# Decoder layer kernel: how the masks of the adapter attention are added, and in which order its passes run

## The chip, the core and the metric

The kernel runs on one core of one Trainium2 chip. The metric is the device time of one execution in microseconds (us). The kernel before takes 1193.47 us, the median of three runs (1193.44 to 1193.86).

## The reference

Three post-norm blocks over x, 16 sequences ("batches") of 128 tokens by 256 features, all in float32: layer A (causal self-attention with 16 heads), layer B (self-attention with 32 heads of 8 features under an additive mask, plus gated attention to a second input of the same shape), and block C/D (attention with 16 heads of 128, then four experts). The change touches layer B:

```
scores = (q @ k.T) * inv_sqrt_d + attention_mask      # mask: one 128x128 float32 array per batch, 0 or -1e9
scores = maximum(scores, finfo.min)
w = softmax(scores);  attn = w @ v
a = tanh(gate) * softmax(q @ a_k.T * inv_sqrt_d);  attn = attn + a @ a_v     # no mask here
x = layernorm(x + attn @ Wo)
```

## The kernel before

**Engines and waits.** Each engine runs a list of instructions written out in order (pe_ab, dve_ab, act_ab, pool_ab, sp_ab) and waits on semaphores. Nothing is reordered: the lists are generated by a loop over steps s, and tables (xts, projs, masked, clamps, ends, tos, turned ...) say in which step each piece of background work stands.

**Units and passes.** A unit is four heads: a score tile of 128 x 4 x 128 in one PSUM bank. Layer A has 64 units, layer B 256 (numbers n = 64 to 319). A batch of layer B has 16 units: eight of self-attention with the mask (kd = 0), then eight on the second input (kd = 1). Units go in pairs, one pair in every second step. In this text a step is named by s modulo 16, so a batch has the pair steps 0, 2, ... 14, and steps 0 to 6 hold its masked units in the first pass. Two batches make a chunk (number c); layer B has chunks 8 to 15.

*Pass 1* computes the scores on TensorE (L554) into bank 0 or 1 (bank n % 2), and VectorE takes the row maxima of each bank (`maxima`, L737). A unit's first write waits for the maxima two units earlier (m_dve). *Pass 2*, 28 steps later, computes the transposed scores with the maxima subtracted through extra rows of the operands (L589) into bank 2 or 3 (`bank2`). In masked units VectorE adds the transposed mask and writes the sum to SBUF (`mask2`, L746), and ScalarE takes the exponential there (L978); in the others ScalarE reads the bank (L985). `pv`, two steps after pass 2, multiplies by the values: 16 matmuls for a pair, each 32 columns wide, on four column tiles (L611).

**The mask.** A chunk's mask is loaded in float32, clamped (L729) and split into a high part (ScalarE, L963) and a rest (GpSimd, L1090). Pass 1 of a masked unit begins with two matmuls of a 128x128 identity by 512 mask columns (L547), one for each part. The mask turned by TensorE (L512) and copied by ScalarE (L935) serves `mask2`.

**Small products.** Turned maxima ("sh": L565, then the copy L971 by ScalarE), turned outputs ("to": L621, after the copy L997), projections and output products (L472 to L474) share banks 6 and 7 alternately from step s = 86 on: `home[key] = bank[6 + len(home) % 2]`. Before it writes, `turn` waits until the last user of that bank has been read.

**Order in a step.** TensorE: pass 1, pass 2, pv, small products. VectorE: maxima, divide (L766 to L777) and other outputs, L723, then the two `mask2`, then residual and statistics (L801, L695 to L699).

## Time and profile before

| what | value |
|---|---|
| median of three runs | 1193.47 us |
| profiled execution, first to last instruction (its own time) | 1193.7 us |
| TensorE busy in it | 1128.8 us (95%) |
| VectorE busy | 993.6 us (83%) |
| ScalarE, GpSimd busy | 660.4 us, 656.9 us (55% each) |
| mean granted TensorE clock | 0.990 |
| packets of the sync engine's DMA queue, share of 16 engines | 23.1% |

Layer A runs to about 175 us, layer B from there to about 556 us, C and D to the end. No time around the span is given for the profiled execution, so its span is its own time here. Matmuls are pipelined, and a listed duration of one contains a fixed part that overlaps with its neighbours: what a matmul costs in a row of them is the distance of starts. Idle time of an engine that nothing later waits for costs nothing.

### The profile page before, as it was taken

The page shows a single profiled execution, that of the slowest core. Times are in us where ns is not written, and L with a number is a line of the kernel's source. Part 1 is how long each engine was busy: PE and PEld are TensorE (multiplying, and loading weights), DVE is VectorE, ACT ScalarE, POOL GpSimd, SP SyncE. Part 2 cuts the span into 40 slices and gives each one's busy share as a digit, 9 for nine tenths or more (in the row PEclk, how much of TensorE's full clock was granted, in tenths as well). Part 3 has the DMA queues.
Part 4 walks back from the last instruction along what each step waited for, and adds up shares of the span by engine and source line. Part 5 has one row for each costly group of instructions (what it writes and reads, how often), then busy time and mean ns, then how long its engine had stood idle before and what let it go on. Part 6 is the DMA issues. An engine that isn't in the chain of part 4 may idle for free.

```text
span 1193.7 us, 29551 instructions
## 1 busy us (share of the span) xinstructions
PE 1128.8 (95%) x11172; PEld 934.4 (78%) x11172; DVE 993.6 (83%) x2284; ACT 660.4 (55%) x1687; POOL 656.9 (55%) x706
## 2 busy tenths in 40 slices
PE   5899999899999999879999999999999999999997
PEld 5667666666776766546899899998999899997887
DVE  6768887888889898978888888888888888877977
ACT  5466554566766667565555444444444444558663
POOL 4467655545455455254778544544554454847665
PEclk9899999999999999999999999999999999999999
DMA  6875443334333433212222000000000100101111
GB/s 161 205 186 135 122 125 87 87 95 116 88 106 101 106 97 97 76 58 76 68 63 63 1 1 2 1 1 2 1 1 1 37 1 1 37 18 37 36 36 36
DMA packets 98670, 76.68 MB, mean 64 GB/s; under 512 B 73547, under 2 KB 86987, under 8 KB 98529
## 3 DMA queue, kind: packets, MB, share of 16 engines
q1 hardware_dynamic: 98529, 74.80, 23.1%
q8 instruction: 89, 1.46, 0.5%
q14 instruction: 52, 0.43, 0.1%
HBM read 53.86 MB, written 19.92 MB: 62 GB/s over the span
## 4 chain that ended last, share of the span: by engine, by line
PE 58%; DVE 23%; issue 7%; ACT 5%; POOL 3%; SPq 2%; DMA 2%; DVEq 0%; POOLq 0%; ACTq 0%
PE bank L1518 5%; DVE B_nr L737 4%; PE bank L1519 4%; PE bank L1520 4%; PE bank L1574 4%; PE bank L1547 4%; PE bank L611 4%; DVE PT L746 3%; PE bank L472 2%; PE bank L554 2%; SPq L1154 2%; PE bank L1534 2%; PE bank L1589 2%; PE bank L1587 2%; PE bank L1588 2%
## 5 line engine op out<-in xcount | busy, mean ns | idle before, releaser
L1822 POOL TENSOR_TENSOR C_QK<-C_t1b,C_t2b 128x512 f32<-128x512 f32 x128 | 168.9, 1320 | 226.6 <-DVE C_t2b L1661 226.0
L1658 DVE SCALAR_TENSOR_TENSOR C_t1b<-bank,C_bcol,C_tabs 64x512 f32<-64x512 f32 x256 | 192.0, 750 | 37.3 <-PE bank L1520 33.2
L737 DVE TENSOR_REDUCE B_nr<-bank 128x4 f32<-128x512 f32 x256 | 164.4, 684 | 22.6 <-PE bank L554 21.0
L1518 PE MATMUL bank<-C_XTh,C_Wh 128*128 128x512 f32 x256 | 111.9, 437 | 4.4 <-DVE C_t2b L1661 1.9
L985 ACT ACTIVATE PT<-bank 128x512 f32<-128x512 f32 x160 | 92.2, 598 | 39.8 <-PE bank L589 39.3
L1754 ACT ACTIVATE C_P<-bank,C_nm 128x128 f32<-128x128 f32 x256 | 90.7, 367 | 34.0 <-DVE C_nm L1671 32.4
L978 ACT ACTIVATE PT<-PT 128x512 f32<-128x512 f32 x96 | 59.3, 630 | 88.7 <-DVE PT L746 88.7
L1773 ACT ACTIVATE C_V<-bank 128x512 f32<-128x512 f32 x64 | 38.1, 597 | 124.1 <-PE bank L1536 122.5
L611 PE MATMUL bank<-PT,vpool 128*32 128x128 f32 x2048 | 97.4, 285 | 4.3 <-ACT PT L978 3.1
L1519 PE MATMUL bank<-C_XTl,C_Wh 128*128 128x512 f32 x256 | 101.2, 395 | 0.0
L1520 PE MATMUL bank<-C_XTh,C_Wl 128*128 128x512 f32 x256 | 100.8, 394 | 0.0
L1661 DVE SCALAR_TENSOR_TENSOR C_t2b<-bank,C_bcol,C_tabs 128x512 f32<-128x512 f32 x128 | 96.1, 751 | 1.8
L554 PEld LDWEIGHTS bank<-stk 48*128 48x128 bf16 (+1 forms) x1280 | 50.9, 96 | 52.3 <-issue 27.5
L554 PE MATMUL bank<-stk 48*128 48x128 bf16 (+1 forms) x1280 | 77.7, 221 | 9.6 <-DVE B_nr L737 8.9
L589 PE MATMUL bank<-stk 54*128 54x128 bf16 (+1 forms) x1280 | 76.5, 219 | 10.0 <-DVE PT L746 3.8
L1762 ACT ACTIVATE C_OTh<-bank,C_bcol 128x512 fp32r<-128x512 f32 x64 | 44.1, 690 | 73.6 <-PE bank L1574 73.0
L1682 DVE SCALAR_TENSOR_TENSOR C_OTl<-bank,C_bcol,C_OTh 128x512 fp32r<-128x512 f32 x64 | 47.9, 748 | 38.9 <-ACT C_OTh L1762 38.8
L705 POOL TENSOR_TENSOR rstd<-ve,mhalf 128x1 f32<-128x1 f32 x48 | 28.1, 584 | 91.1 <-DVE ve L699 91.1
L589 PEld LDWEIGHTS bank<-stk 54*128 54x128 bf16 (+1 forms) x1280 | 53.5, 95 | 27.8 <-DVE PT L746 6.8
L1534 PE MATMUL bank<-C_Wh,C_XTh 128*128 128x256 f32 x256 | 72.5, 283 | 1.6 <-DVE C_t2b L1661 1.3
L1587 PE MATMUL bank<-C_Wh,C_OTh 128*128 128x256 f32 x256 | 72.0, 281 | 0.4 <-DVE C_OTl L1682 0.4
L1535 PE MATMUL bank<-C_Wl,C_XTh 128*128 128x256 f32 x256 | 71.9, 281 | 0.0
(267 smaller groups left out, 3683.5 us busy)
## 6 DMA issues: line engine op xcount, KB each, us to landing
Adrq<-PB SPq DMA_DIRECT2D x16, 192.0 KB, 3.2
Adrk<-PB SPq DMA_DIRECT2D x16, 192.0 KB, 3.4
...
```

Source lines behind the costliest of these rows:

```text
L554: m = e.matmul(bank[n % 2][:, j * 128:j * 128 + 128], QS[L][i3][rows, h, :], (AS if kd else KS[L])[i3][rows, h, :], start=bool(kd), stop=b ...
L589: m = e.matmul(bank2(n)[:, j * 128:j * 128 + 128], (AS if kd else KS[L])[i3][rows, h, :], QS[L][i3][rows, h, :], start=bool(L), stop=bool( ...
L611: m = e.matmul(o[32 * j:32 * j + 32, c3 * 128:c3 * 128 + 128], vp[:, h, :], pt_of(n)[:, j * 128:j * 128 + 128], start=first or not L, stop ...
L737: e.tensor_reduce(dst, bank[n % 2][:, :].rearrange("p (a b) -> p a b", a=4), AX.X, ALU.max, negate=True).then_inc(sem("m_dve"), 1)
L1518: e.matmul(o[:, :], CWh[hp][:, cs], XCh[0][:, t, :], start=t == 0, stop=False)
L1519: e.matmul(o[:, :], CWh[hp][:, cs], XCl[0][:, t, :], start=False, stop=False)
L1520: m = e.matmul(o[:, :], CWl[hp][:, cs], XCh[0][:, t, :], start=False, stop=t == 1)
L1534: e.matmul(ob, XCh[0][:, t, xs], CWh[hp][:, cs], start=t == 0, stop=False)
L1587: e.matmul(o, OCh[:, bs], CWh[hp][:, cs], start=r == 0 and b % 2 == 0, stop=False, skip_group_check=True)
L1658: e.scalar_tensor_tensor(out=v4(t1b[kq][lo:lo + 64, :]), in0=v4(o[hi:hi + 64, :]), scalar=bc[hi:hi + 64, :], in1=tabsC[hi:hi + 64, 2 * kq ...
L1661: e.scalar_tensor_tensor(out=v4(t2b[kq][:, :]), in0=v4(o[:, :]), scalar=bc, in1=tabsC[:, 2 * kq, :].unsqueeze(1).to_broadcast([128, 4, 128 ...
L1822: e.tensor_tensor(QK[v % 3][:, kq, :], t1b[kq][:, :], t2b[kq][:, :], ALU.add).then_inc(sem("rc_pool"), 1)
```

## The change

The mask of pass 1 is split into three bf16 parts (MQ) instead of two float32 parts. They are written to DRAM and read back by rows (MP): 96 partitions, three parts of 32 rows, four groups of rows. A unit's mask is then four matmuls with a 96x32 selection matrix (`pick`), each with 512 moving columns and each into its own 32 output partitions of the bank. The same is done with the three parts turned (MTQ, MTP) for pass 2, and only in the first unit of each pair (t = 0, even n). The odd unit (t = 1) is still added by VectorE. ScalarE now reads even masked units from the bank. The preparation of a chunk has two copies by ScalarE and two subtractions by GpSimd in place of one each, six more transposes on TensorE with a copy of 768 elements by ScalarE, and four DMAs. The turned maxima go in two DMAs for a batch instead of four.

From s = 64 on TensorE's order in a step is pv, mask of pass 2, masks of pass 1, pass 2, pass 1, small products. Pass 2 comes 26 steps after pass 1 instead of 28 and pv stays at 30. VectorE does `mask2` (odd unit) ahead of the maxima of the step. `mask_turns` puts the transposes of the mask parts ("mp") in step 5 for chunks 10 to 15, among the users of banks 6 and 7.

```diff
-    MKh = [sb(f"B_MKh{i}", [128, 2, 128], F32R, st_ab) for i in range(2)]
-    MKl = [sb(f"B_MKl{i}", [128, 2, 128], F32R, st_ab) for i in range(2)]
+    MP = [sb(f"B_MP{i}", [96, 4, 2, 128], BF16, st_ab) for i in range(2)]
...
+    pick = sb("B_pick", [96, 32], BF16, st_ab)
+    MQ = sb("B_MQ", [128, 3, 2, 128], BF16, st_ab)
+    MR = sb("B_MR", [128, 2, 128], F32, st_ab)
+    MTP = [sb(f"B_MTP{i}", [96, 4, 2, 128], BF16, st_ab) for i in range(2)]
+    MTQ = sb("B_MTQ", [128, 3, 2, 128], BF16, st_ab)
...
-    LAST_FIRST = 292
+    LAST_FIRST = 294
...
+    def is_masked(n):
+        return n >= NA and unit(n)[2] == 0
+
+    def adds_mask(n):
+
+        return is_masked(n) and unit(n)[3] == 1
...
-        return [s - 12] if 12 <= s < NA + 12 else pair(s - 28)
+        return [s - 12] if 12 <= s < NA + 12 else pair(s - 26)
...
+    mask_parts = [{s + k: c for s, c in clamps.items()} for k in (1, 2, 3, 4)]
+    masks_out = {s + 5: c for s, c in clamps.items()}
+    mask_turns = {s + (1 if c < 10 else 3): c for s, (c, _) in masked.items()}
+    masks_t_out = {bg0(c) + 28: c for c in range(8, 16)}
...
+        def mask_parts_turned(c):
+            q.wait_ge("mq_pool", 2 * (c - 7))
+            o = turn(("mp", c), "mt_act", 2 * (c - 7))[:, :].bitcast(BF16)
+            for part in range(3):
+                for b in range(2):
+                    k = 2 * part + b
+                    m = e.transpose(o[:, k * 128:k * 128 + 128], MQ[:, part, b, :], identb[:, :])
             m.then_inc(sem("mt_pe"), 1)
...
+        def mask_by_rows(o, parts, b):
+
+            for g in range(4):
+                e.matmul(o[32 * g:32 * g + 32, :].rearrange("p (a b) -> p a b", a=4), pick[:, :],
+                         parts[0:96, g, b, :].unsqueeze(1).to_broadcast([96, 4, 128]), start=True, stop=False, skip_group_check=True)
+
+        def mask1(n):
+            b = unit(n)[1]
+            c = 8 + b // 2
+            if n >= 2:
+                q.wait_ge("m_dve", n - 1)
+            q.wait_ge("ld_B", 48)
+            q.wait_ge(*parts_ready("mp_in", c))
+            mask_by_rows(bank[n % 2], MP[c % 2], b % 2)
+
+        def mask2(n):
+            b = unit(n)[1]
+            c = 8 + b // 2
+            bank2_free(n)
+            q.wait_ge("ld_B", 48)
+            q.wait_ge(*parts_ready("mtp_in", c))
+            mask_by_rows(bank2(n), MTP[c % 2], b % 2)
...
-                elif not kd:
-                    q.wait_ge("identr", 1)
-                    q.wait_ge("mkl_pool", b // 2 + 1)
-                    for k, part in enumerate((MKh, MKl)):
-                        e.matmul(scores, identr[:, :], part[(b // 2) % 2][:, b % 2, :].unsqueeze(1).to_broadcast([128, 4, 128]),
-                                 start=k == 0, stop=False, skip_group_check=True)
...
         for s in steps:
+            if s >= NA:
+                for n in pv_units(s):
+                    pv(n)
+                for n in pass2_units(s):
+                    if is_masked(n) and not adds_mask(n):
+                        mask2(n)
+                for n in pass1_units(s):
+                    if is_masked(n):
+                        mask1(n)
+                if pass2_units(s):
+                    pass2(pass2_units(s))
             if pass1_units(s):
                 pass1(pass1_units(s))
-            if pass2_units(s):
-                pass2(pass2_units(s))
-            for n in pv_units(s):
-                pv(n)
+            if s < NA:
+                if pass2_units(s):
+                    pass2(pass2_units(s))
+                for n in pv_units(s):
+                    pv(n)
...
             if s in CHANGE:
                 outputs()
+            for n in pass2_units(s):
+                if adds_mask(n):
+                    mask2(n)
             for n in pass1_units(s):
                 maxima(n)
...
-            for n in pass2_units(s):
-                if n >= NA and unit(n)[2] == 0:
-                    mask2(n)
...
+        def mask_part(c, part):
             q.wait_ge("clamp", c - 7)
-            if c >= 10:
-                q.wait_ge("s_pe", last_unit(2 * (c - 2) + 1, 0) + 1)
-            e.activation(MKh[c % 2][:, :, :], MK[c % 2], ACT.Copy).then_inc(sem("mkh_act"), 1)
+            if part == 0:
+                if c > 8:
+                    q.wait_ge(*parts_ready("mp_in", c - 1))
+                    q.wait_ge("mt_pe", 2 * (c - 8))
+                e.activation(MQ[:, 0, :, :], MK[c % 2], ACT.Copy).then_inc(sem("mq_act"), 1)
+            else:
+                q.wait_ge("mq_pool", 2 * (c - 8) + 1)
+                e.activation(MQ[:, 1, :, :], MR[:, :, :], ACT.Copy).then_inc(sem("mq_act"), 1)
...
+        def mask_out(c):
+
+            q.wait_ge("mq_pool", 2 * (c - 7))
+            q.wait_ge("mp_in", 32 * (c - 8))
+            load(mask_dram[0], MQ[:, :, :, :].rearrange("p j b k -> p (j b k)"), "mp_in")
...
+        def mask_rows(c):
+
+            q.wait_ge("mp_in", 32 * (c - 8) + 16)
+            if c >= 10:
+                q.wait_ge("s_pe", last_unit(2 * (c - 2) + 1, 0) + 1)
+            load(MP[c % 2][:, :, :, :].rearrange("p g b k -> p g (b k)"), by_rows(mask_dram[0]), "mp_in")
...
```

**TensorE, steps 4 and 6 of a batch, before.** B_nmb is the shift (maxima in parts), OTf the outputs to turn, B_MKh and B_MKl the mask parts, stk the operands of L554 (pass 1) and L589 (pass 2).

```order
L565 MATMUL bank<-identb,B_nmb 96x128 [waits ab_act,sh_pool]
L565 MATMUL bank<-identb,B_nmb 96x128
L621 MATMUL bank<-ident,OTf 128x128 [waits mt_act,ot_act]
L621 MATMUL bank<-ident,OTf 128x128 x2
L547 MATMUL bank<-B_MKh,B_identr 128x512 [waits m_dve]
L547 MATMUL bank<-B_MKl,B_identr 128x512
L547 MATMUL bank<-B_MKh,B_identr 128x512 [waits m_dve]
L547 MATMUL bank<-B_MKl,B_identr 128x512
L554 MATMUL bank<-stk 128x128 x8
L589 MATMUL bank<-stk 128x128 [waits e_act]
L589 MATMUL bank<-stk 128x128 x7
L611 MATMUL bank<-PT,vpool 32x128 x8
```

After the two turns come the masks, pass 1, pass 2 and pv of step 6.

**TensorE, the same place in the kernel after, in a batch that prepares a mask.** B_MQ are the mask parts to turn, B_MP those read back by rows; L641 is pass 2, L602 pass 1, L663 pv.

```order
L673 MATMUL bank<-ident,OTf 128x128 [waits mt_act,ot_act]
L673 MATMUL bank<-ident,OTf 128x128 x2
L543 MATMUL bank<-identb,B_MQ 128x128 [waits sh_act,mq_pool]
L543 MATMUL bank<-identb,B_MQ 128x128 x5
L663 MATMUL bank<-PT,vpool 32x128 x8
L560 MATMUL bank<-B_MP,B_pick 32x512 [waits m_dve]
L560 MATMUL bank<-B_MP,B_pick 32x512 x3
L560 MATMUL bank<-B_MP,B_pick 32x512 [waits m_dve]
L560 MATMUL bank<-B_MP,B_pick 32x512 x3
L641 MATMUL bank<-stk 128x128 [waits e_act]
L641 MATMUL bank<-stk 128x128 x7
L602 MATMUL bank<-stk 128x128 x8
```

The transposes of B_MQ stand between the turned outputs of step 4 and pv of step 6 and wait for ScalarE's copy of the turned maxima (sh_act), since they use the same bank; everything of step 6 has moved behind them, and pass 1 is the last of its step.

**VectorE, from the maxima of step 8 to the adds of step 12, before.** B_nr<-bank is the maxima of a pair, PT<-bank,stk and stk<-bank,stk are mask adds.

```order
L737 TENSOR_REDUCE B_nr<-bank 128x4 x2
L723 TENSOR_TENSOR XTl<-bank,XTh 128x512
L737 TENSOR_REDUCE B_nr<-bank 128x4 x2
L791 TENSOR_TENSOR OTl<-bank,OTh 128x256
L729 TENSOR_SCALAR stk<-stk 128x256
L737 TENSOR_REDUCE B_nr<-bank 128x4 x2
L746 TENSOR_TENSOR PT<-bank,stk 128x512 x2
```

**VectorE, the same place after.**

```order
L803 TENSOR_REDUCE B_nr<-bank 128x4 x2
L789 TENSOR_TENSOR XTl<-bank,XTh 128x512
L812 TENSOR_TENSOR PT<-bank,stk 128x512
L803 TENSOR_REDUCE B_nr<-bank 128x4 x2
L857 TENSOR_TENSOR OTl<-bank,OTh 128x256
L795 TENSOR_SCALAR stk<-stk 128x256
L812 TENSOR_TENSOR stk<-bank,stk 128x512
L803 TENSOR_REDUCE B_nr<-bank 128x4 x2
```

Each masked pair of pass 2 has one add instead of two; it stands between L789 (formerly L723) or L857 (formerly L791) and the maxima of its step.

## Rows read from the trace of the kernel before

**Rows 1.** The page: busy us (share of the span) and instructions by engine.
```profile
PE 1128.8 (95%) x11172; PEld 934.4 (78%) x11172; DVE 993.6 (83%) x2284; ACT 660.4 (55%) x1687; POOL 656.9 (55%) x706
```

**Rows 2.** Busy time by stretch: length, then busy us of each engine, clock, DMA.
```profile
386.70:429.80 43.10, 41.76 (x648) 30.09 (x647) 38.52 (x76) 29.52 (x77) 22.45 (x30) 1.00 0.38 102
473.00:516.00 43.00, 37.83 (x596) 24.63 (x594) 39.13 (x83) 25.54 (x62) 11.90 (x19) 0.96 0.32 90
```

**Rows 3.** Groups by line: shapes, count | busy us, mean ns of one | idle before, releaser.
```profile
L737 DVE TENSOR_REDUCE B_nr<-bank 128x4 f32<-128x512 f32 x256 | 164.4, 684 | 22.6 <-PE bank L554 21.0
...
L547 PE MATMUL bank<-B_MKh,B_identr 128*128 128x512 f32 x128 | 57.1, 446 | 1.1 <-DVE B_nr L737 1.0
...
L746 DVE TENSOR_TENSOR PT<-bank,stk 128x512 f32<-128x512 f32 x96 | 62.6, 680 | 1.2 <-PE bank L589 1.2
```

**Rows 4.** Timeline of DVE, one batch of layer B: start us, length us, engine, line.
```profile
388.07 1.28 DVE L737 TENSOR_REDUCE B_nr<-bank 128x4 f32<-128x512 f32 x2
...
390.58 1.28 DVE L737 TENSOR_REDUCE B_nr<-bank 128x4 f32<-128x512 f32 x2
392.22 0.69 DVE L723 TENSOR_TENSOR XTl<-bank,XTh 128x512 fp32r<-128x512 f32 x1 [0.36 <-ACT XTh L888]
392.83 1.28 DVE L737 TENSOR_REDUCE B_nr<-bank 128x4 f32<-128x512 f32 x2
...
394.67 1.29 DVE L737 TENSOR_REDUCE B_nr<-bank 128x4 f32<-128x512 f32 x2 [0.23 <-PE bank L554]
...
397.12 0.42 DVE L801 TENSOR_TENSOR z<-bank,X 128x256 f32<-128x256 f32 x1
...
398.32 1.28 DVE L737 TENSOR_REDUCE B_nr<-bank 128x4 f32<-128x512 f32 x2
...
401.19 1.29 DVE L737 TENSOR_REDUCE B_nr<-bank 128x4 f32<-128x512 f32 x2 [0.40 <-PE bank L554]
...
403.63 1.29 DVE L737 TENSOR_REDUCE B_nr<-bank 128x4 f32<-128x512 f32 x2
...
406.30 1.29 DVE L737 TENSOR_REDUCE B_nr<-bank 128x4 f32<-128x512 f32 x2 [0.19 <-PE bank L554]
...
409.13 1.29 DVE L737 TENSOR_REDUCE B_nr<-bank 128x4 f32<-128x512 f32 x2
```

**Rows 5.** Timeline of PE in the same batch, around a masked step.
```profile
396.92 0.28 PE L472 MATMUL bank<-XTh,B_Wh 128*128 128x256 f32 x1
...
397.27 0.28 PE L472 MATMUL bank<-XTh,B_Wh 128*128 128x256 f32 x1
...
402.54 0.50 PE L547 MATMUL bank<-B_MKh,B_identr 128*128 128x512 f32 x1
...
408.14 0.40 PE L547 MATMUL bank<-B_MKh,B_identr 128*128 128x512 f32 x1
408.37 0.40 PE L547 MATMUL bank<-B_MKl,B_identr 128*128 128x512 f32 x1
408.70 0.40 PE L554 MATMUL bank<-stk 48*128 48x128 bf16 x8
408.93 0.39 PE L589 MATMUL bank<-stk 54*128 54x128 bf16 x8
409.25 0.65 PE L611 MATMUL bank<-PT,vpool 128*32 128x128 f32 x16
409.83 0.55 PE L621 MATMUL bank<-ident,OTf 128*128 128x128 f32 x3
```

**Rows 6.** Timeline of ACT, and PE's wait for it, where the shift is turned.
```profile
386.24 1.07 ACT L985 ACTIVATE PT<-bank 128x512 f32<-128x512 f32 x2
...
388.09 0.38 ACT L971 ACTIVATE B_nmT<-bank 96x256 bf16<-96x256 bf16 x1
...
388.62 0.52 PE L621 MATMUL bank<-ident,OTf 128*128 128x128 f32 x3 [0.18 <-ACT B_nmT L971]
```

**Rows 7.** Timeline of the sync engine: start and length of four DMA issues.
```profile
388.63 3.06 SPq L1154 DMA_DIRECT2D stk<-B_nmT  x4
```

More of the change, by code:

```diff
@@ L126, in program @@
                for i in range(2)] for k in RW[L]} for L in range(2)]
-    tabs_ready = ("ld_A", 32), ("ld_B", 16)
+    mask_dram = [nc.dram_tensor(f"Bmask{i}", [128, 768], BF16, kind="Internal").ap() for i in range(2)]
+    by_rows = lambda a: a.rearrange("(g r) (j x) -> (r j) g x", g=4, j=3)
+    tabs_ready = ("ld_A", 32), ("ld_B", 48)
     ot = I["c_one"]
     NA, NN = 64, 320
-    LAST_FIRST = 292
+    LAST_FIRST = 294
     def unit(n):
@@ L220, in pass2_units @@
     def pass2_units(s):
-        return [s - 12] if 12 <= s < NA + 12 else pair(s - 28)
+        return [s - 12] if 12 <= s < NA + 12 else pair(s - 26)
     def pv_units(s):
-        return pass2_units(s - 2)
-    STEPS = NN + 28 + 2 + 12
+        return [s - 14] if 14 <= s < NA + 14 else pair(s - 30)
+    STEPS = NN + 30 + 12
     AHEAD = 20
@@ L570, in pass2 @@
                 L, b, kd, t, i, hs = unit(n)
[L571 to L578 removed]
+                bank2_free(n)
                 if not L:
[L580 removed]
+                    q.wait_ge("consts", 1)
                     e.matmul(bank2(n)[:, :].rearrange("p (a b) -> p a b", a=4), identb[:, :],
@@ L588, in pass2 @@
                     rows, h = (slice(64 * t, 64 * t + 54), hs[j] % 16) if L else (slice(0, 99), hs[j])
+                    alone = bool(L) and (adds_mask(n) or not is_masked(n))
                     m = e.matmul(bank2(n)[:, j * 128:j * 128 + 128], (AS if kd else KS[L])[i3][rows, h, :], QS[L][i3][rows, h, :],
-                                 start=bool(L), stop=bool(L) or j == 3, skip_group_check=not L)
+                                 start=alone, stop=alone or j == 3, skip_group_check=not alone)
                     if j == 3:
@@ L975, in exps @@
             L, b, kd, t, i, hs = unit(n)
-            if L and kd == 0:
+            if adds_mask(n):
                 q.wait_ge("mt_dve", v_masked(n))
@@ L1037, in act_ab @@
                 masks(masked[s - 1][0])
-                mask_high(masked[s - 1][0])
+            if s - 1 in mask_turns:
+                mask_parts_turned(mask_turns[s - 1])
+            for part in range(2):
+                if s in mask_parts[2 * part]:
+                    mask_part(mask_parts[2 * part][s], part)
             if s - 1 in vals:
@@ L1118, in pool_ab @@
                 add_adapter(tos[s - 2][0])
-            if s - 2 in masked:
-                mask_low(masked[s - 2][0])
+            for part in range(2):
+                if s in mask_parts[2 * part + 1]:
+                    mask_rest(mask_parts[2 * part + 1][s], part)
             for part in range(2):
@@ L1199, in shift @@
             for hg in range(1 + L):
-                for kd in range(NK[L]):
-                    row = 64 * hg + 48 + 3 * kd if L else 96
-                    load(QS[L][b % (5 if L else 10)][row:row + 3, :, :], nmT[L][b % 2][48 * hg:48 * hg + 48, kd, :],
-                         shift_sem(g)[0])
+                row = 64 * hg + 48 if L else 96
+                load(QS[L][b % (5 if L else 10)][row:row + 3 * NK[L], :, :], nmT[L][b % 2][:, hg, :], shift_sem(g)[0])
         def ones_rows(i):
@@ L1266, in sp_ab @@
                 stack_in(c, ti, b)
+            if s in masks_out:
+                mask_out(masks_out[s])
+            if s - 2 in masks_out:
+                mask_rows(masks_out[s - 2])
+            if s in masks_t_out:
+                mask_t_out(masks_t_out[s])
+            if s - 2 in masks_t_out:
+                mask_t_rows(masks_t_out[s - 2])
             if s in parts:
```

101 lines of the change are left out of this document (62 added, 39 removed).

## Prediction

> **What bounds the kernel now.** The page comes first: TensorE is busy for 95% of the span and VectorE for 83% [rows 1], so both matter, and a sum over the whole says little. The windows come next, one chunk of layer B long: 43.10 us, VectorE busy for 38.52, TensorE for 41.76 at full clock, ScalarE for 29.52 [rows 2]. The reader is to see that ScalarE and GpSimd have room and that neither of the other two fills its chunk. The groups then give prices: 128 mask adds of 680 ns on VectorE, 256 maxima of 684 ns, 128 pairs of mask matmuls [rows 3]. Last come the timelines, since the two engines wait for each other within a step. I write D(r) for the start of the maxima in step r, and measure a step by D to D. The batch of [rows 4], from step 6 on, reads 2.51, 2.25, 1.84, 3.65, 2.87, 2.44, 2.67, 2.83: 21.06 us. The chunk's other batch has what is left of 43.10: 22.04.
>
> Distances of starts on TensorE [rows 5]: mask matmul 0.23; masks to pass 1 0.33, thus 0.10 for the change of kind; pass 1 to pass 2 0.23; pass 2 to pv 0.32; pv 0.58; six projection matmuls 0.71 (three take 0.35). Pass 1 starts 0.43 before its D (408.70 to 409.13). A masked unit's first write waits for a bank that maxima must leave: for the second unit this is D + 1.35 (402.54 against 401.19). In the masked steps VectorE and TensorE so form one loop: mask of the second unit, pass 1, maxima. Maxima and adds follow each other at 0.60 (two maxima of 1.28 overlap their successor by 0.08).
>
> **The masks of pass 1.** 256 matmuls of 512 columns go, 0.93 us a pair (4 x 0.23), and 512 come on four column tiles. The price of four together is not in the trace. From below it is one stream, 0.235; from above four, 0.94. The nearest row is pv, 16 matmuls of 128 columns on four column tiles in 0.58; at the projections' rate (0.12 for 256 columns) they would take 0.94 one after another, and a 128-wide float32 matmul is hardly cheaper than that rate. So tiles overlap, and as the short ones are also held by their issue (0.036 each), I take 0.235, 0.47 a pair. The Trainium skill (TensorE: Matmul & The Clock Gate, Part 3: Packing small matmuls) gives three 32-column tiles of 512 columns a speedup of 2.38, not 3; by that four would cost about 0.30, an estimate from that page, and the sum would be some 5 us worse. No row here has 512 columns on such tiles.
>
> **The order of step 0 to 6.** The mask becomes cheaper, but pass 2 now stands between it and pass 1. Loop: 1.35 + 0.24 (second mask) + 0.10 + 0.23 (pass 2) + pass 1 and latency 0.43 = 2.34. Before, the same loop was 1.35 + 0.47 + 0.10 + 0.43 = 2.34 too. What is won is only where TensorE or the adds were the bound: steps 2, 4 and 6 took 2.44, 2.67 and 2.83, and become 2.34 each. The Trainium skill (TensorEngine Tiling, PSUM Bottleneck) says that tiling speeds up TensorE but not the emptying of PSUM. These steps agree: the loop waits on maxima, and by its rule alone halving the mask would win nothing.
>
> **The adds.** 64 of 128 go, 0.60 each on VectorE, 4.8 a chunk. In exchange each of the remaining 64 stands between pass 2 and the maxima of its step, and each pair has a mask on TensorE (0.24). Step by step, with pass 2's result 0.40 after its start:
> - Step 8: TensorE has small products, pv 0.58, pass 2, pass 1: 2.43 (before 2.51).
> - Step 10: the subtraction L723 cannot start before D(8) + 1.57 (before 1.64 [rows 4]). Then come add 0.60 and maxima, where before the maxima came at once: 2.77 (before 2.25).
> - Step 12: pv 0.58, mask 0.24 and pass 2 now lie before pass 1; the add ends 0.40 later than pass 1 would allow: 2.2 with six projection matmuls in front, 2.86 with twelve (before 1.84 here).
> - Step 14: before, VectorE had maxima 1.20, two adds 1.20 and the residual chain (397.12 to D at 398.32) 1.20. Now one add less, 3.0, where twelve matmuls stand in front. Where 18 do, as here, TensorE sets it: 2.13 + 0.58 + 0.24 + 0.23 + 0.24 + gaps, with the add 3.66 (before 3.65).
> - Step 0: both masks and the add: 1.35 + 0.24 + 0.10 + 0.40 + 0.60 = 2.70 (before 2.87).
>
> The batch shown becomes 20.8 (2.43 + 2.77 + 2.2 + 3.66 + 2.70 + 3 x 2.34), the other 20.8 also. Gain 0.3 and 1.2, 1.5 a chunk, 12 us over eight chunks.
>
> **The turned parts.** This is the costly edit. In step 5 the transposes of the mask parts need the bank that the turned maxima have just filled, so TensorE waits for ScalarE's copy L971, and pv, masks, pass 2 and pass 1 of step 6 are queued behind. ScalarE comes to that copy only after two exponentials, a split and the outputs: 388.47 - 386.24 = 2.23 from the first exponential, and TensorE goes on 0.15 later [rows 6]. Before, the next user of that bank stood behind a whole step's work. The exponentials can start 0.20 after pass 1 of step 4 starts. So: 0.20 + 2.23 + 0.15 = 2.58, six transposes and change 0.49, pv 0.58, two masks 0.48, change 0.10, pass 2 0.23: pass 1 of step 6 starts 4.46 after that of step 4, not 2.34. That is 2.1 us in each of chunks 11 to 15, 10.5 in all. In chunk 10 the bank's last user is an output product, and I take nothing. Cost bounds: 0, if ScalarE is done earlier, and 3.3 a time (a pair of exponentials later, 1.2).
>
> **The end of layer B.** In the last two batches few projections remain, VectorE is busy for 39.13 of 43.00 [rows 2], and fewer adds count more fully: 3 us beyond the above, and 2 us after the last maxima, where the remaining passes of 26 steps have half the adds (estimates; bounds 0 and 10 together).
>
> **The rest.** ScalarE gets about 1.3 us a chunk more and GpSimd 0.7: both hide in idle time (13 and 20 us a chunk [rows 2]); uncovered they would cost 8 x 2.0. The sync engine has four issues more and four fewer a chunk at 0.77 (3.06 for four [rows 7]): nothing. Layer A and C: nothing.
>
> **Sum.** 1193.7 - 12 - 3 - 2 + 10.5 = 1187.2. The span is 0.2 above the median, within the runs; I forecast **1187 us**.
>
> **Rivals.**
> - *The turn does not wait* (ScalarE is ahead, since even exponentials no longer wait for adds): the 10.5 fall away, 1176.7. For it: ScalarE idles 31% of the chunk. Against: the copy stands behind exponentials of the same step, which can't be early.
> - *Even.* The steps' gain is as in the batch shown, 0.3, in all 16, 4.8 in place of 12, and the end gives 3: 1196.4 with the full wait, 1193 with two thirds of it.
> - *Slower: the shift rows arrive late.* Pass 2 of a batch begins at step 10, not 12. The copy of the maxima ends 2.4 after pass 1 of step 4, and pass 2 of step 10 starts at about 2.34 + 2.43 + 2.08 = 6.85: 4.4 us for two issues (1.53) and the landing. Before it had 6.0 (from 388.47 to 394.67 - 0.43 + 0.23). It decides when the landing takes more than 2.7, or when six loads in front (3.8) hold the queue. Price 1.2 in eleven batches without the turn's wait, 13 us: 1200. For it: no slack by these numbers. Against: two issues in place of four, 1.5 earlier.
> - *The column tiles don't overlap*: 0.94 for four. Masked steps grow by 0.34 + 0.70, the mask of pass 2 by 0.70: 4 x 1.04 + 4 x 0.70 = 7 us a batch, 112 in all, 1299. pv speaks against it.
>
> **Chances.** Forecast 0.42 (own range 1181 to 1191), no wait 0.17, even 0.15, late rows 0.22, no overlap 0.04. Within 0.2% (1191.1 to 1195.9, about what a measurement can tell from no change) lie most of the even case and the edge of the forecast: 0.17. Faster 0.56, slower 0.27. The range 1174 to 1203 leaves out 0.1 on either side.
>
> **What would show it.** Starts of the four mask matmuls a few hundredths apart and the next group 0.24 later; masked steps at 2.34; step 10 at 2.8 with the add after L723; a wait of TensorE of about 2 us for ScalarE's copy of the maxima, five times; 64 adds. Wrong would be: no such wait, chunks under 41 us, or TensorE waiting for the DMA of the shift rows.

## The result: slower, and the profile after

The changed kernel takes 1204.29 us (median of four runs, 1202.52 to 1208.75) against 1193.55 for the kernel before beside it (1193.44 to 1193.86): ratio 1.009, interval 1.0068 to 1.0113. The forecast was 1187, so the sign is wrong, and the time lies outside the range of 1174 to 1203.

The profiled execution spans 1204.0 us. The page, as in [rows 1]:

```profile
PE 1121.0 (93%) x11732; PEld 924.7 (77%) x11732; DVE 956.0 (79%) x2219; ACT 670.9 (56%) x1703; POOL 660.9 (55%) x714
```

TensorE and VectorE both do less than before, and the kernel is slower: the time went into waits. The groups, as in [rows 3]:

```profile
L803 DVE TENSOR_REDUCE B_nr<-bank 128x4 f32<-128x512 f32 x256 | 164.4, 684 | 52.7 <-PE bank L602 52.1
...
L560 PE MATMUL bank<-B_MP,B_pick 96*32 96x512 bf16 x512 | 49.0, 402 | 17.4 <-DVE B_nr L803 17.1
...
L560 PE MATMUL bank<-B_MTP,B_pick 96*32 96x512 bf16 x256 | 26.4, 393 | 1.0 <-DVE B_nr L803 0.8 <-ACT PT L1062 0.3
...
L812 DVE TENSOR_TENSOR PT<-bank,stk 128x512 f32<-128x512 f32 x32 | 22.1, 691 | 11.9 <-PE bank L641 11.8
L812 DVE TENSOR_TENSOR stk<-bank,stk 128x512 f32<-128x512 f32 x32 | 22.1, 690 | 17.2 <-PE bank L641 16.7
```

The maxima now idle 52.7 us for pass 1, 22.6 before. To find where, I take D(0) of each batch of layer B, the start of the maxima of its step 0, all from the VectorE timelines. Batch lengths in us:

| batch | 0 | 1 | 2 | 3 | 4 | 5 | 6 | 7 | 8 | 9 | 10 | 11 | 12 | 13 | 14 | 15 to its last D |
|---|---|---|---|---|---|---|---|---|---|---|---|---|---|---|---|---|
| before | 31.1 | 20.4 | 21.0 | 22.1 | 21.5 | 21.7 | 21.4 | 21.8 | 21.4 | 21.7 | 21.4 | 21.7 | 21.4 | 21.1 | 20.7 | 18.4 |
| after | 32.0 | 26.1 | 20.2 | 23.3 | 20.7 | 24.1 | 20.7 | 24.1 | 20.7 | 25.4 | 20.7 | 22.6 | 20.7 | 21.5 | 18.9 | 16.7 |

The last maxima start at 525.9 before and 536.3 after: 10.4 us, the whole difference of the spans (10.3). The even batches are 0.7 shorter. The loss is batch 1 (+5.7) and the six odd batches 3 to 13 (+10.9 together), and 1.8 before batch 1.

One odd batch, VectorE's maxima, which answers to [rows 4] (start, length, then what it waited for in brackets):

```profile
389.84 1.28 DVE L803 TENSOR_REDUCE B_nr<-bank 128x4 f32<-128x512 f32 x2
392.17 1.29 DVE L803 TENSOR_REDUCE B_nr<-bank 128x4 f32<-128x512 f32 x2 [1.04 <-PE bank L602]
394.50 1.29 DVE L803 TENSOR_REDUCE B_nr<-bank 128x4 f32<-128x512 f32 x2 [1.04 <-PE bank L602]
400.32 1.29 DVE L803 TENSOR_REDUCE B_nr<-bank 128x4 f32<-128x512 f32 x2 [2.64 <-PE bank L602]
403.90 1.29 DVE L803 TENSOR_REDUCE B_nr<-bank 128x4 f32<-128x512 f32 x2 [1.48 <-PE bank L602]
```

Steps 0 to 4 go at 2.33, then one step takes 5.82 and the next 3.58. TensorE in the same place, as in [rows 5, 6]:

```profile
394.08 0.39 PE L602 MATMUL bank<-stk 48*128 48x128 bf16 x8
394.39 0.31 PE L613 MATMUL bank<-identb,B_nmb 128*96 128x128 bf16 x2
394.54 0.50 PE L673 MATMUL bank<-ident,OTf 128*128 128x128 f32 x3
396.66 0.80 PE L543 MATMUL bank<-identb,B_MQ 128*128 128x128 bf16 x6 [1.62 <-ACT B_nmT L1048]
397.39 1.08 PE L663 MATMUL bank<-PT,vpool 128*32 128x128 f32 x16
398.24 1.08 PE L560 MATMUL bank<-B_MP,B_pick 96*32 96x512 bf16 x8
399.25 0.61 PE L641 MATMUL bank<-stk 54*128 54x128 bf16 x8
399.65 0.64 PE L602 MATMUL bank<-stk 48*128 48x128 bf16 x8
```

ScalarE beside it, the first exponential and the copy that TensorE waits for:

```profile
394.27 0.60 ACT L1062 ACTIVATE PT<-bank 128x512 f32<-128x512 f32 x1 [0.46 <-PE bank L641]
...
396.13 0.38 ACT L1048 ACTIVATE B_nmT<-bank 96x256 bf16<-96x256 bf16 x1
```

From pass 1 (394.08) to the turned parts (396.66) it is 2.58 us: the wait that the prediction worked out, to the hundredth, and part by part (0.19 to the first exponential, 2.24 from there to the end of the copy, 0.15 to TensorE). But the transposes then take 0.73 up to pv in place of 0.49, and pv 0.85 in place of 0.58. The windows say why (length, busy us of PE, PEld, DVE, ACT, POOL, then the granted clock, DMA share, GB/s):

```profile
389.80:392.20 2.40, 1.58 (x33) 0.80 (x26) 1.36 (x4) 1.41 (x3) 2.18 (x6) 1.00 0.51 155
394.50:398.00 3.50, 1.88 (x23) 1.45 (x27) 3.11 (x6) 2.52 (x6) 1.95 (x3) 0.75 0.83 200
398.00:402.00 4.00, 4.00 (x45) 2.90 (x35) 1.65 (x4) 1.91 (x4) 0.91 (x2) 0.50 0.21 63
402.00:406.00 4.00, 4.00 (x76) 2.71 (x75) 2.43 (x6) 2.67 (x10) 0.73 (x1) 0.87 0.64 148
```

From 396.25 on, still in the standstill, the granted clock is 0.50, the 1.2 GHz level, and TensorE runs at it until about 403. Batch 11 of the same execution has the same wait and keeps its clock:

```profile
442.73 0.49 PE L543 MATMUL bank<-identb,B_MQ 128*128 128x128 bf16 x6 [1.61 <-ACT B_nmT L1048]
443.16 0.64 PE L663 MATMUL bank<-PT,vpool 128*32 128x128 f32 x16
443.62 0.62 PE L560 MATMUL bank<-B_MP,B_pick 96*32 96x512 bf16 x8
444.17 0.40 PE L641 MATMUL bank<-stk 54*128 54x128 bf16 x8
```

There the step takes 4.25, where 2.33 is the undisturbed one, and in batch 13 too. In batches 3, 5, 7 and 9 it takes 5.4 to 5.8. So the wait costs 1.9 us by itself, and in batch 9, with the clock behind it and the step after it, 4.7.

### The profile page after: what moved, and what is told of

Its sections match the earlier page's. It is cut to its first block, busy times and chain, and to the rows that moved or that the text cites. A ratio compares the mean times of both kernels' runs of the same rounds, so it can differ in the third digit from the quotient of the medians.

```text
span 1204.0 us, 30629 instructions
## 1 busy us (share of the span) xinstructions
PE 1121.0 (93%) x11732; PEld 924.7 (77%) x11732; DVE 956.0 (79%) x2219; ACT 670.9 (56%) x1703; POOL 660.9 (55%) x714
## 4 chain that ended last, share of the span: by engine, by line
PE 65%; DVE 18%; issue 6%; SPq 4%; ACT 3%; DMA 2%; POOL 2%; POOLq 0%; DVEq 0%; ACTq 0%
PE bank L663 5%; PE bank L1632 5%; PE bank L1633 4%; PE bank L1634 4%; PE bank L1688 4%; PE bank L1661 4%; DVE B_nr L803 4%; SPq L1237 4%; PE bank L641 4%; PE bank L494 3%; PE bank L560 3%; PE bank L602 2%; PE bank L1648 2%; PE bank L495 2%; PE bank L496 2%
## 5 line engine op out<-in xcount | busy, mean ns | idle before, releaser
L803 DVE TENSOR_REDUCE B_nr<-bank 128x4 f32<-128x512 f32 x256 | 164.4, 684 | 52.7 <-PE bank L602 52.1
L1062 ACT ACTIVATE PT<-bank 128x512 f32<-128x512 f32 x224 | 130.2, 597 | 106.4 <-PE bank L641 104.9
L663 PE MATMUL bank<-PT,vpool 128*32 128x128 f32 x2048 | 98.6, 289 | 2.0 <-ACT OTf L1072 2.0
L641 PEld LDWEIGHTS bank<-stk 54*128 54x128 bf16 (+1 forms) x1280 | 49.4, 96 | 48.0 <-issue 36.0
L602 PE MATMUL bank<-stk 48*128 48x128 bf16 (+1 forms) x1280 | 77.4, 221 | 3.3 <-DVE B_nr L803 2.5
L641 PE MATMUL bank<-stk 54*128 54x128 bf16 (+1 forms) x1280 | 77.3, 223 | 2.5 <-DMA stk<-A_nmT 2.1
L462 POOL TENSOR_TENSOR PB<-y,PB 128x512 bf16<-128x512 f32 x36 | 42.6, 1183 | 56.1 <-ACT PB L994 55.9
L1650 PE MATMUL bank<-C_Wh,C_XTl 128*128 128x256 f32 x256 | 71.9, 281 | 0.0
```

The lines of the kernel that those rows point to most:

```text
L602: m = e.matmul(bank[n % 2][:, j * 128:j * 128 + 128], QS[L][i3][rows, h, :], (AS if kd else KS[L])[i3][rows, h, :], start=bool(kd), stop=b ...
L641: m = e.matmul(bank2(n)[:, j * 128:j * 128 + 128], (AS if kd else KS[L])[i3][rows, h, :], QS[L][i3][rows, h, :], start=alone, stop=alone o ...
L663: m = e.matmul(o[32 * j:32 * j + 32, c3 * 128:c3 * 128 + 128], vp[:, h, :], pt_of(n)[:, j * 128:j * 128 + 128], start=first or not L, stop ...
L803: e.tensor_reduce(dst, bank[n % 2][:, :].rearrange("p (a b) -> p a b", a=4), AX.X, ALU.max, negate=True).then_inc(sem("m_dve"), 1)
L1062: e.activation(pt_of(n)[:, :], bank2(n)[:, :], ACT.Exp).then_inc(sem("e_act"), 1)
```

## The experiments

Each set ran on a chip of its own, where the kernel before took 1193.4 to 1194.2 us at the median of each set (1191.5 to 1198.3 singly); so kernels are compared by their ratios to it.

Theory W: two waits for a shared PSUM bank, and the half clock behind them, are the loss. Rivals: C, the clock falls in these batches whatever the waits; O, odd batches are long for their other work.

**The turned parts moved: e1, e2, e3.** Small products take the two spare banks in turn, in the order of the program. With the turned parts in step 15 both neighbours of the bank are a step or more away. e1 moves chunks 10 to 15, e2 chunk 9, e3 both:

```
-    mask_turns = {s + (1 if c < 10 else 3): c ...}
+    mask_turns = {s + (1 if c < 9 else 8 if c == 9 else 13): c ...}      # e3
-    masks_t_out = {bg0(c) + 28: c ...}
+    masks_t_out = {bg0(c) + (28 if c < 9 else 36): c ...}                # e3
```

> Changed kernel, with the turned parts of chunks 10 to 15 taken from step 5 to step 15 of the odd batch (ten steps later, their DRAM legs eight steps later), where the bank they take was left a step or more before; all the work is the same. Theory W (the wait for the bank in step 5, and the half clock behind it, is the loss): the odd batches 3, 5, 7, 9, 11 and 13 of the changed kernel took 23.3, 24.1, 24.0, 25.4, 22.6 and 21.5, 140.9 us together; without the wait they take the 20.7 of the even ones (the last 19 to 20), about 124, so the kernel takes 1204.3 - 16 = 1188 us (1185 to 1191), step 4 to 6 takes 2.3 us in place of 4.2 to 5.8, and the mean granted clock rises from 0.98 to above 0.985. Rival C (the clock falls in the odd batches whether PE waits there or not, because the new stage leaves it too little to do): only the 2.1 us of the wait go in six batches, 1204.3 - 12 = 1192, with 0.5 still in the windows after step 4. Rival O (the odd batches are long for their other work): 1202 to 1205.

Measured: 1193.52 us (10 runs), ratio 0.9994 [0.9974, 1.0015], profiled clock 0.985. Odd batches 3 to 13: 20.5, 21.7, 21.7, 21.7, 21.7, 20.3, together 127.6 in place of 141.0. The wait is gone, and the granted clock reads 1.00 in all six, which O and C exclude. The time itself, 1193.5, is nearer to C's 1192 than to W's 1188, so it is the profile that decides. W's number was not reached since step 4 to 6 takes 3.1 in five of the batches, not 2.3 (below), and step 14 to 0 takes 3.05, not 2.74, where the six transposes now stand.

> Changed kernel, with the turned parts of chunk 9 alone moved, from step 8 to step 15 of batch 1 (DRAM legs eight steps later). Theory W: in the changed kernel they took the bank that chunk 9's last value product had before, so that product (step 9) got the bank of the xt product of step 8 and waits for DVE's XTl (1.08 us idle before L494 at 222.59), and passes 2 and 1 of step 10 stand behind it. With the move batch 1 takes 21 to 22 us in place of 26.2: 1199.5 us (1197.5 to 1201). Rival C (step 8 to 14 of batch 1 runs at a low clock in the kernel before too, 0.85 and 0.58 from 220 to 226, so it is the clock and not the bank): 1203 to 1204.5.

Measured: 1203.78 us (4 runs), ratio 1.0077 [1.0052, 1.0101]. The time lies in C's range and misses W's. Batch 1 takes 22.5 in place of 26.1 in the profile, which speaks for W; the same profile starts layer B 2.7 us later (180.7 against 178.0), in code that is the same in both. Against the changed kernel's own ratio of 1.009 the gain is not resolved. This trace also repeats the untouched wait of step 5: the clock falls behind it in batches 5, 7, 9 and 11 and not in 3 and 13.

> Changed kernel with both moves: turned parts of chunks 9 to 15 in step 15. Theory W: both gains add, 1204.3 - 16 - 5 = 1183 us (1180 to 1187), faster than the kernel before by 0.5 to 1.1 per cent. Rival C: 1191 or above, mean granted clock still 0.98. Rival O: 1200 or above.

Measured: 1189.62 us (7 runs), ratio 0.9952 [0.9931, 0.9972], faster than the kernel before. Batch 1 takes 24.2 in its profile, and the value product of step 9 (L494 at 218.25) no longer waits. Right in direction, 7 us short of 1183. By the ratios the two moves together are worth 1.38% (1.009 to 0.9952), 16.5 us; this is what the turned parts cost as they stood.

**The wait put into the kernel before: e4.**

```
             if s >= TURNED_FIRST:
                 turns(s)
+            if s in turned and turned[s] in (20, 22, 24, 26, 28):
+                q.wait_ge("sh_act", turned[s] + 1)
```

> Kernel before, with nothing but one wait more: after the turn of the shift rows in step 4 of batches 5, 7, 9, 11 and 13, TensorE waits for ScalarE's copy of them (nmT, which ends at 388.5 in batch 9, while TensorE went on with the masks of step 6 at 386.06). Theory W: TensorE stands still for 2.2 us there, the maxima of step 6 come 2.0 us later (390.1 in place of 388.1), five times: 1193.5 + 10 = 1203.5 us at an unchanged clock, and up to 1209 if the granted clock falls to 0.5 behind the wait as in the changed kernel (then the step takes 6 us or more, and the mean clock is lower). Rival (the wait is covered by DVE, which sets the end in this kernel, and the loss of the changed kernel has another cause): 1193 to 1196.

Measured: 1207.92 us (4 runs), ratio 1.0117 [1.0095, 1.0138]. One wait in five batches, nothing else, costs 14 us, within W's range for a clock that falls. TensorE in batch 7, and the windows around it:

```profile
343.41 0.50 PE L621 MATMUL bank<-ident,OTf 128*128 128x128 f32 x3
346.13 0.50 PE L547 MATMUL bank<-B_MKh,B_identr 128*128 128x512 f32 x1 [2.22 <-ACT B_nmT L973]
...
348.24 1.08 PE L611 MATMUL bank<-PT,vpool 128*32 128x128 f32 x16
```
```profile
342.40:346.50 4.10, 1.88 (x31) 1.21 (x31) 3.00 (x6) 3.67 (x9) 2.48 (x3) 1.00 0.11 25
346.50:351.50 5.00, 5.00 (x61) 3.83 (x59) 2.16 (x5) 1.92 (x6) 2.35 (x3) 0.66 0.42 93
```

Batches 5, 7 and 11 take 25.4, batches 9 and 13 23.9 and 22.9; the kernel before has 21.7, 21.8, 21.7, 21.7 and 21.1. In batch 7 the clock falls at about 347.3, 1.1 us after TensorE has gone on. So about 2 us of wait without a clock fall, 3.7 with one, in a kernel without the masks' column tiles. This is the clearest case for the mechanism.

**TensorE kept busy in the wait: e5.** Changed kernel, wait untouched:

```
             if s in mask_turns:
+                for n in pass1_units(s + 1) if mask_turns[s] >= 10 else ():
+                    for _ in range(4):
+                        mask1(n)
                 mask_parts_turned(mask_turns[s])
```

> Changed kernel with the wait in step 5 left as it is, and TensorE given something to do in it: the eight mask matmuls of the next pair (0.47 us) are issued four times over ahead of the turned parts of chunks 10 to 15, into the first-pass banks that the real ones overwrite right after. They can start once the maxima of step 4 are read, about 1.1 us into the 2.6 us of the wait, and end with it. They add 1.9 us of work to a stretch in which TensorE stood still. Theory W (the clock falls because TensorE stood still): with 1.1 us of standing in place of 2.6 the clock stays up, step 4 to 6 takes 4.2 to 4.5 in place of 5.4 to 5.8, the odd batches take 22.6 like number 11 of the profiled run, and the kernel with more work in it is the faster: 1204.3 - 6 = 1198 us, clock above 0.985. Rival L (the clock falls because of the load of the column tiles and transposes, not the standstill): 1204 to 1208, windows behind the wait at 0.5 as before. Rival A (the additional matmuls simply add up): 1204.3 + 6 x 1.9 = 1216.

Measured: 1201.93 us (8 runs), ratio 1.0055 [1.0035, 1.0075], against 1.009 [1.0068, 1.0113] without the additional work: more matmuls, and no more time but 0.35% less, about 4 us; the intervals overlap a little. The profile is plainer: step 4 to 6 takes 4.7 in all six odd batches.

```profile
391.75 1.91 PE L560 MATMUL bank<-B_MP,B_pick 96*32 96x512 bf16 x32 [0.21 <-DVE B_nr L806]
393.59 0.51 PE L543 MATMUL bank<-identb,B_MQ 128*128 128x128 bf16 x6
394.03 0.65 PE L663 MATMUL bank<-PT,vpool 128*32 128x128 f32 x16
```
```profile
391.00:394.50 3.50, 3.29 (x61) 1.88 (x65) 3.12 (x6) 2.38 (x6) 1.94 (x3) 1.00 0.68 182
394.50:398.50 4.00, 4.00 (x78) 3.03 (x68) 2.55 (x6) 3.28 (x11) 1.65 (x2) 1.00 0.26 54
```

The clock stays at 1.00 in all six, where it fell in four of six in each of the two traces with the bare wait (the changed kernel's and e2's). So it is the standstill and not the kind of work that lets it fall. The filler outlasts the wait by a few tenths (4.7, not 4.2 to 4.5), and batch 1 was as long as in the changed kernel (26.1): 1198 was too low.

**The same for batch 1: e6.** e3 with twelve 128-column matmuls, identity by identity, behind each pair step from s = 84 to 92, into a bank that nobody uses there.

> Kernel e3_both_late (1189.6 us), with twelve idle matmuls (identity by identity, 128 columns, 0.7 us together) behind each of the pair steps 4, 6, 8, 10 and 12 of batch 1, where TensorE waits for the scores' maxima and runs at half clock for 8 us afterwards (batch 1 took 24.2 us there, steps 12 to 14 alone 4.9). They go to a bank that nobody uses there. Theory W: the clock stays at 1.0 in batch 1, which takes 21.5 us: 1187 us. Rival A: their 3.5 us add up: 1193.

Measured: 1189.46 us (10 runs), ratio 0.9955 [0.9939, 0.9972], as e3. In its profile the clock is 1.00 in all of batch 1, as W has it, but the batch takes 22.7 and not 21.5, and e9 below, without filler and with a clock of 0.65 in its step 12 to 14, has 22.7 too. So what the filler gives is not shown; only that its 3.5 us don't add up is.

**Which part of the change gives what: e7, e8, e10, e11.** All four have e3's two moves. Diffs in short: e7 `adds_mask` is true for all masked units (and the counts of adds doubled); e8 puts mask, pass 1, mask, pass 2, pv in that order on TensorE; e10 does both, with the lag of 28 and VectorE's old order; e11 calls `mask1(n)` twice.

> Kernel e3_both_late with the half of the change that concerns the second pass undone: DVE adds the mask to both units of a masked pair again (0.6 us each, as L746 did before) and no column tile is written to a second-pass bank; the turned parts are still made, and the order of the passes and the first pass's column tiles stay. It tells what DVE's relief is worth. Theory D (in the masked steps DVE's 2 maxima and 2 masks, 2.5 us, and not TensorE, set the step): masked steps take 2.55 in place of 2.33 us, and 2.8 where DVE has other work: 14 batches x 4 x 0.3 = 17 us more, 1205 us or so. Rival P (TensorE's work is what sets the masked steps; the gain came from the float32 mask matmuls replaced in the first pass): 1187 to 1192.

Measured: 1231.55 us (4 runs), ratio 1.0301 [1.027, 1.0332]. More than theory D allowed. In batch 9 the four steps from 8 to 0 take 3.2, 2.7, 3.6 and 3.3 against 2.7, 2.2, 3.8 and 3.1 in e3, 1.1 more; and in steps 0 to 6 the clock reads 0.50 to 0.74 and they take 1.6 more (the mean clock of the run is 0.965, e3's 0.990). I had put the adds into the wrong steps: pass 2 lags 26, so they stand ahead of the maxima of steps 10 to 0.

> Kernel e3_both_late with the order inside a step put back: first-pass masks and scores first, then second-pass masks and scores, then PV; nothing else. It tells what the new order is worth. Theory D: the maxima need the first pass, and DVE comes to them right after the two masks... the first pass is ready earlier, so nothing is lost and nothing won while DVE sets the step: 1187 to 1192. Rival Q (the new order lets PV and masks fill the time in which the banks of the first pass are being read; in the old order TensorE stands before the mask matmuls for the maxima, at the head of its queue, with PV behind): masked steps 0.2 to 0.5 us longer, 1200 to 1215.

Measured: 1278.47 us (4 runs), ratio 1.0695 [1.065, 1.074]; both theories were far off. Steps 8 to 14 take 3.8 to 4.1 each. VectorE there:

```profile
410.53 0.69 DVE L812 TENSOR_TENSOR PT<-bank,stk 128x512 f32<-128x512 f32 x1 [0.74 <-PE bank L663]
411.14 1.28 DVE L803 TENSOR_REDUCE B_nr<-bank 128x4 f32<-128x512 f32 x2
...
414.34 0.69 DVE L812 TENSOR_TENSOR stk<-bank,stk 128x512 f32<-128x512 f32 x1 [1.39 <-PE bank L663]
414.94 1.28 DVE L803 TENSOR_REDUCE B_nr<-bank 128x4 f32<-128x512 f32 x2
```

The add stands ahead of the maxima on VectorE and waits for pv (L663), which frees its buffer and is last on TensorE now; the maxima wait behind it, though their scores are there. I had undone one half of a change of order that VectorE and TensorE share. These steps are longer than e3's by 4.5 us a batch, 68 of the 93 us that layer B is longer by in the profiles; most of the rest is the clock, 0.50 to 0.83 in many of the steps 2 to 6. Where it is at 1.00 a masked step takes 2.10 in this run, against 2.33 in e3: pass 2 no longer stands between the masks and pass 1, and the 0.23 that the prediction's loop gives it is what goes.

> The first-pass half of the change alone: bf16 masks by way of DRAM and column tiles write the first-pass banks, while the order of the passes, the lag of 28 steps and DVE's masks on both units of the second pass are those of the kernel before (the turned parts are made, late, and used by nobody). TensorE loses four float32 matmuls (0.93 us) and gains eight short ones (0.47) in each of 64 masked steps. Theory D (DVE and the round trip of the banks, not TensorE's load, set the steps of the kernel before): at most 5 us: 1188 to 1194. Rival P (TensorE's load sets them): 0.3 to 0.46 us in most of 64 steps, 1165 to 1178.

Measured: 1193.58 us (10 runs), ratio 0.9997 [0.9984, 1.0011]: theory D. Cheaper masks on TensorE alone are worth nothing that can be told in the time. The masked steps that VectorE sets take 2.39, its two maxima and two adds at 0.60. In the profile something is won, 0.2 us in even and 0.6 in odd batches (21.2 and 21.1 in batches 4 to 11), 5.3 from batch 2 to 15; the start and batch 1 are 3.5 longer, at a lower clock (mean 0.982 against 0.990), and take most of it back.

> Kernel e3_both_late with the eight column-tile matmuls of the first pass issued twice in each of 64 masked steps (the second write replaces the first). It prices TensorE's load in the masked steps (2.33 us each). Theory P (TensorE is what sets the step of 2.33 now: PV, masks, pass 2, masks, pass 1 one behind the other): 64 x 0.47 = 30 us more, 1219 us. Rival B (the trip from scores over maxima back to the bank sets it, and PV and second-pass work leave TensorE gaps of 0.2 to 0.3): 64 x 0.2 = 13 us, 1203.

Measured: 1204.78 us (4 runs), ratio 1.0091 [1.0071, 1.0111], 1.39% or 17 us over e3 (1203 was rival B's). The masked steps take 2.55 in place of 2.33: of 0.47 us more in a step 0.22 shows, rival B. It is the 0.23 of one unit, as the prediction's loop has it, in which only the second unit's mask stands.

**The step that was still long: e9.** VectorE in e3, step 4 of batch 9, and GpSimd beside it:

```profile
381.75 1.29 DVE L803 TENSOR_REDUCE B_nr<-bank 128x4 f32<-128x512 f32 x2 [1.04 <-PE bank L602]
382.95 0.37 DVE L832 RECIPROCAL rr<-bank 128x36 f32<-128x36 f32 x1
383.36 1.05 DVE L836 TENSOR_TENSOR rr<-rr,B_tg 128x36 f32<-128x36 f32 x1
384.44 0.49 DVE L843 TENSOR_TENSOR ON<-bank,rr 128x192 f32<-128x192 f32 x2
384.85 1.28 DVE L803 TENSOR_REDUCE B_nr<-bank 128x4 f32<-128x512 f32 x2
```
```profile
383.20 1.16 POOL L459 TENSOR_TENSOR y<-ab,PB 128x512 f32<-128x512 f32 x1 [0.90 <-ACT PB L991]
```

A product of 36 columns takes 1.05 us and ends with GpSimd's instruction (384.41 and 384.36). e9 gives it a PSUM operand:

```
-            e.reciprocal(r12, v12[:, :, 24:27])
+            first = o[:, 384:420] if kd else rr[:, :]
+            e.reciprocal(first..., v12[:, :, 24:27])
...
-                e.tensor_tensor(rr[:, :], rr[:, :], tg[:, :], ALU.mult)
+                e.tensor_tensor(rr[:, :], first, tg[:, :], ALU.mult)
```

> Kernel e3_both_late (1189.6 us), with DVE's reciprocal of the adapter's denominators written to 36 free PSUM columns beside the product and read from there by the product with the gate (L836), in place of an SBUF operand. In e3 that product of 36 columns took 1.05 us in step 4 of batches 5, 7, 9, 11 and 13 and ended each time together with a POOL tensor_tensor (383.20 + 1.16 against 383.36 + 1.05), while its median over 16 is 198 ns; the maxima of step 6 stood behind it (step 4 to 6 took 3.1 us, 2.3 in the even batches). Theory G (a DVE operation with two SBUF operands waits out POOL's, one with a PSUM operand does not): the product takes 0.2 to 0.3 us, step 4 to 6 takes 2.3 to 2.4, five times 0.75: 1189.6 - 3.8 = 1185.8 us. Rival (the 1.05 us has another reason, or TensorE is late there anyhow, with its first pass of step 6 ready at 384.05): no change, 1188 to 1191.

Measured: 1185.48 us (6 runs), ratio 0.9928 [0.991, 0.9946]; forecast 1185.8. VectorE and GpSimd now:

```profile
381.28 0.38 DVE L833 RECIPROCAL bank<-bank 128x36 f32<-128x36 f32 x1
381.70 0.20 DVE L837 TENSOR_TENSOR rr<-bank,B_tg 128x36 f32<-128x36 f32 x1
381.93 0.49 DVE L844 TENSOR_TENSOR ON<-bank,rr 128x192 f32<-128x192 f32 x2
382.41 1.29 DVE L803 TENSOR_REDUCE B_nr<-bank 128x4 f32<-128x512 f32 x2
```
```profile
381.53 1.16 POOL L459 TENSOR_TENSOR y<-ab,PB 128x512 f32<-128x512 f32 x1 [0.90 <-ACT PB L992]
```

GpSimd's instruction runs just the same, and the product takes 0.20 in the middle of it. Step 4 to 6 is 2.3, and the odd batches 5 to 11 take 20.9. The intervals of e3 and e9 overlap (0.9931 to 0.9946), so the 4 us rest on the profile, five steps of 3.1 that are 2.3 now.

In the kernel before this product is held up next to GpSimd too, 0.88 in each of batches 5, 7, 9, 11 and 13, so it could take this repair as well, and no run tries that. Batch 9 before:

```profile
386.75 0.88 DVE L770 TENSOR_TENSOR rr<-rr,B_tg 128x36 f32<-128x36 f32 x1
```
```profile
386.42 1.16 POOL L440 TENSOR_TENSOR PB<-y,PB 128x512 bf16<-128x512 f32 x1 [2.02 <-ACT PB L929]
```

What the change is worth by itself, with its turned parts out of the way, is therefore e3's 0.5%, and what e9 and e12 have beyond it is the repair.

**All together: e12** (e9 and the filler of e6).

> All repairs together: e3_both_late, the filler of e6_late_filled in batch 1, and the denominators by way of PSUM of e9. Theories W and G: e9's gain of 3.8 us and up to 1.5 us of the filler (batch 1 took 22.7 us in e6's profile, 24.2 in e3's, though the medians of the two did not differ): 1189.6 - 4.5 = 1185 us, 0.7 per cent under the kernel before. Rival: 1189, as e6.

Measured: 1183.95 us (6 runs), ratio 0.9918 [0.9902, 0.9935]; forecast 1185. It is 0.8% under the kernel before and the fastest here; whether the filler has a part in it the intervals of e9 and e12 don't tell. One chunk of it:

```profile
353.60:395.20 41.60, 39.35 (x724) 27.89 (x716) 33.16 (x68) 30.87 (x78) 22.88 (x31) 1.00 0.49 128
```

41.60 in place of 43.10 [rows 2]. That is the prediction's 1.5 us a chunk, but only with the repair of e9, which the prediction did not have: in e3 the same chunk takes 42.5.

## Why the prediction was wrong

The mechanism was right and its size was not: the term that failed is **the turned parts**, 10.5 us, 4.46 for step 4 to 6 in five chunks. They cost 16.5 us (e3), for TensorE's clock fell behind the wait, chunk 10 had it too, and chunk 9 lost its bank. That is 6 of the 17 us between forecast and measurement. The other 11 are for the most part gains that were forecast and did not come, and what is left of batch 1. By stretches of the profile, after minus before, in us:

| stretch | forecast | measured |
|---|---|---|
| start and chunk 8 (batches 0 and 1), with the turned parts of chunk 9 | -1.5 | +7.4 |
| chunks 9 to 14, the wait of the turned parts aside | -9.0 | -6.9 |
| turned parts of chunks 10 to 15 (measured by taking them away, e1) | +10.5 | +13.4 |
| the last two batches | -4.5 | -3.5 |
| after the last maxima | -2.0 | -0.1 |
| sum | -6.5 | +10.3 |

- *Column tiles*, 0.235 for four: right. Eight take 0.55 with the change of kind (443.62 to 444.17), so four take 0.22, and the later masks of batch 9 the same; the four of a unit start 0.007 apart and the next four 0.22 later. pv's matmuls start in fours too, 0.11 from one four to the next (443.40, 443.51), so it is not the issue of each that makes them 0.036. The Trainium skill's 2.38 for three tiles (TensorE: Matmul & The Clock Gate, Part 3: Packing small matmuls) is not what this kernel shows: these tiles overlap fully, as far as starts tell.
- *Steps 0 to 6*, 2.34: right, 2.33, wherever nothing else disturbs them in batches 4 to 14. The loop itself is shown by e11 (every mask twice, 0.22 of 0.47 seen) and e8 (pass 2 out of the loop, 2.10). Before, it was rather VectorE's four instructions, 4 x 0.60, that set 2.44, as the 2.39 of e10, with masks as cheap as here, suggests.
- *Batch of 20.8*: right for the even ones (20.7), and step by step: 2.32, 2.62, 2.27, 3.70 and 2.74 from step 6 of an odd batch to step 0 of the next, where 2.43, 2.77, 2.2, 3.66 and 2.70 were forecast. The 64 adds are there. The gain of 1.5 a chunk was not right: in e3 it is 0.7, since step 4 to 6 of the odd batch, below, is in no step of [rows 4].
- *The wait of the turned parts*, 2.58: right in place and length. Its price was wrong three times. I charged what follows at full clock; the clock was 0.50 in a part of it in four of six batches, 5.4 to 5.8 in place of 4.46, and in batch 9 in the next step too (3.58). At full clock, in batches 11 and 13, it is 4.25. I took nothing in chunk 10; the bank waits there for the residual addition (1.56 for z), and batch 3 has its 5.4 as well. And chunk 9's turned parts I did not price, below. e1 takes 13.4 us out of the six batches of the profile, e4 puts 14 us into a kernel that never had the change.
- *Chunk 9*: no term at all. Its turned parts are one more product in a row that takes two banks by turns. So the value product of step 9 got the bank of the transposed input of step 8 and waited for VectorE's subtraction:

```profile
222.59 0.58 PE L494 MATMUL bank<-B_Wh,XTh 128*128 128x256 f32 x1 [1.08 <-DVE XTl L789]
222.97 0.41 PE L495 MATMUL bank<-B_Wl,XTh 128*128 128x256 f32 x1
```
  Pass 2 and pass 1 stood behind it, and the clock was at its lower level: L495 is listed with 0.41 where it has 0.28 at full clock. Batch 1 is 5.7 us longer. An inserted product shifts the banks of all that follow, and only the row of banks shows it. With the move, 2 to 4 us of the 5.7 stay; why is open (the kernel before has a slow clock there too).
- *Step 6 of the odd batches*: 2.34 was too low even without the wait. VectorE's outputs with the gate stand there, held by GpSimd (e9), 3.1 in five batches; hidden under the stall, it only showed in e1. Before, the odd batches' step of 3.3 had it too, and I had given [rows 4], in which it is absent, as the pattern of both.
- *The end*: batches 14 and 15 are 3.5 shorter, where 4.5 was expected (their chunk's 1.5 and 3 beyond it). The 2 us after the last maxima didn't come: 667.8 us before, 667.7 after.
- *Rivals*: late shift rows were not seen: pass 2 waits for them 1.1 us in all. "The turn does not wait" would have been 1176.7; e3, which comes nearest to that kernel, takes 1189.6, and e9 1185.5. What its profile, 1185.2 long, has over the forecast is batch 1 (3.7), step 4 to 6 of the odd batches (five times 0.77), the turned parts in step 15 (five times 0.35) and the end (2.6); an earlier start (1.2) and steps a little shorter than forecast take some of it back. "Even" had 0.6 a chunk won in place of 1.5, and without the wait and the repair that is what was measured (0.7), though its own time, 1196.4, was 8 us too low as well.

Added up from the table, after minus before: start of batch 0 0.8, batch 0 0.9, batch 1 5.7, batch 2 -0.8, odd batches 10.9, even ones -3.6, the last two -3.5: 10.4.

What stays open: why one wait is followed by a clock fall and an equal one is not (batches 9 and 11 above; in e2 batch 11 has the fall too); and what is left in batch 1. Of the 1.8 before batch 1 nothing can be said: layer B starts anywhere from 174.6 (e4) to 180.7 (e2) in the profiles. The changed kernel's runs differ by 6 us, but so do those of kernels without the wait (e3 1184.8 to 1192.2, e10 1188.6 to 1195.5), so the waits are not shown to be the reason.
